# A decoder layer on one core: GpSimd's low-part split one step later than ScalarE's rounding, and the cross-attention's pieces spread over three passes

## What is computed

```
q, k, v = x @ Wq, x @ Wk, x @ Wv           # 16 heads of 128
q, k    = rmsnorm(q), rmsnorm(k)
a       = softmax(q @ k.T / sqrt(128) - slope[h] * distance, causal)
y       = rmsnorm(a @ v);   x1 = layernorm(x + concat(y) @ Wproj)
cross   = softmax((ctx @ Wq2.T + bq) @ (ctx @ Wk2.T + bk).T)    # needs the context alone
x2      = layernorm(x1 + x1 @ cross.T)
h       = sigmoid(bit(x2, w_gate)) * bit(x2, w_up);  out = layernorm(x2 + bit(h, w_down))
```

## Time and profile before

| | |
|---|---|
| median of 3 runs | 456.12 us |
| the profiled execution, its own time | 455.92 us |
| its span, first to last instruction | 454.1 us |
| TensorE matmul / weight load busy | 90% / 81% |
| VectorE, ScalarE, GpSimd busy | 71%, 59%, 42% |
| chain of waits, by engine | TensorE 68%, issue 11%, GpSimd 10%, VectorE 6%, ScalarE 2% |

### The profile page before, as it was taken

One profiled execution on the slowest core, in us unless ns is written; L12 is line 12 of the kernel. 1 busy time (PEld: TensorE's weight loads), 2 busy tenths in 40 slices (PEclk: granted clock), 3 DMA queues, 4 the chain that ended last, 5 costly groups with the idle time before them and its releaser, 6 DMA issues.

```text
span 454.1 us, 9089 instructions
## 1 busy us (share of the span) xinstructions
PE 408.9 (90%) x2602; PEld 366.2 (81%) x2612; DVE 320.5 (71%) x1002; ACT 268.7 (59%) x752; POOL 190.1 (42%) x298
## 2 busy tenths in 40 slices
PE   3787999888999999999999999999999999997462
PEld 3666877777899998889999989999999898995221
DVE  2265667676886878887768787877677878973673
ACT  3376756675766646677566466675555567663051
POOL 2536464656444543334435433344345433341201
PEclk9999999999999999999999999999999999999885
DMA  7996535331720333444302443335004444000000
GB/s 215 341 329 221 183 125 210 113 132 69 280 71 0 94 122 136 140 139 133 102 1 70 137 131 113 117 133 162 1 7 141 135 139 139 3 14 12 0 1 23
DMA packets 28736, 52.62 MB, mean 116 GB/s; under 512 B 2576, under 2 KB 22288, under 8 KB 28688
## 3 DMA queue, kind: packets, MB, share of 16 engines
q1 hardware_dynamic: 27968, 52.04, 34.3%
q10 hardware_dynamic: 720, 0.00, 0.1%
HBM read 41.55 MB, written 10.49 MB: 115 GB/s over the span
## 4 chain that ended last, share of the span: by engine, by line
PE 68%; issue 11%; POOL 10%; DVE 6%; ACT 2%; SPq 1%; DMA 1%; POOLq 0%; DVEq 0%; ACTq 0%
PE ps L518 23%; PE ps L571 10%; PE ps L532 5%; PE ps L547 5%; PE ps L538 4%; POOL qk_rstd L378 4%; POOL w_hl L359 4%; PE ps L491 3%; PE ps L552 3%; PE ps L554 3%; PE ps L553 3%; PE ps L546 3%; PE ps L560 2%; POOL y_rstd L386 2%; PE ps L500 2%
## 5 line engine op out<-in xcount | busy, mean ns | idle before, releaser
L518 PE MATMUL ps<-w_hl,xT_hi 128*128 128x384 f32 x512 | 150.9, 376 | 6.3 <-DVE qk_n L750 3.6
L378 POOL TENSOR_TENSOR qk_rstd<-qk_sum,minus_half 128x2 f32<-128x2 f32 x128 | 92.5, 723 | 121.7 <-DVE qk_sum L756 121.3
L518 PEld LDWEIGHTS ps<-w_hl,xT_hi 128*128 128x128 f32 x512 | 91.6, 193 | 14.8 <-issue 9.8
L659 ACT ACTIVATE sq<-ps 128x256 f32<-128x256 f32 x128 | 49.1, 384 | 73.2 <-PE ps L518 71.9
L756 DVE TENSOR_REDUCE qk_sum<-sq 128x2 f32<-128x258 f32 x128 | 53.7, 419 | 49.6 <-ACT sq L659 49.3
L518 PE MATMUL ps<-w_hl,xT_lo 128*128 128x384 f32 x256 | 87.8, 343 | 0.0
L750 DVE TENSOR_TENSOR qk_n<-ps,qk_rstd 128x256 f32<-128x256 f32 x128 | 54.2, 424 | 42.7 <-POOL qk_rstd L378 40.1
L386 POOL TENSOR_TENSOR y_rstd<-y_sum,minus_half 128x2 f32<-128x2 f32 x64 | 47.8, 747 | 67.8 <-DVE y_sum L904 67.8
L571 PE MATMUL ps<-wp,yT 128*128 128x256 f32 x256 | 65.7, 380 | 0.0
L707 ACT ACTIVATE sqy<-ps 128x258 f32<-128x258 f32 x64 | 24.7, 386 | 42.2 <-PE ps L554 42.2
L518 PEld LDWEIGHTS ps<-w_hl,xT_lo 128*128 128x128 f32 x256 | 49.2, 192 | 0.0
(11 more groups left out here) (127 smaller groups left out, 754.6 us busy)
## 6 DMA issues: line engine op xcount, KB each, us to landing
w_hl<-w_store SPq DMA_DIRECT2D x36, 768.0 KB, 4.3
w_store<-w_hl SPq DMA_DIRECT2D x12, 768.0 KB, 4.0
w_raw<-in_L_attn_Wq SPq DMA_DIRECT2D x16, 128.0 KB, 3.0
w_raw<-in_L_attn_Wk SPq DMA_DIRECT2D x16, 128.0 KB, 3.0
w_raw<-in_L_attn_Wv SPq DMA_DIRECT2D x16, 128.0 KB, 3.4
wp<-in_L_attn_Wproj SPq DMA_DIRECT2D x4, 512.0 KB, 6.5
ff_raw<-in_L_ffn_w_gate SPq DMA_DIRECT2D x1, 1024.0 KB, 7.1
ff_raw<-in_L_ffn_w_up SPq DMA_DIRECT2D x1, 1024.0 KB, 9.8
```

The source lines that it names most:

```text
L378: pool.tensor_tensor(qk_rstd[:, t, :], qk_sum[:, t, :], minus_half[:], ALU.pow).then_inc(s_rs[t], 1)
L518: last = pe.matmul(ps[:, t, 0:3 * D], xa[:, k, tok], w_hl[:, place(h), wa, k * 3 * D:(k + 1) * 3 * D], start=(i == 0), stop=(i == len(part ...
L659: act.activation(sq[:, t, :, 0:D], ps[:, t, 0:2 * D].rearrange("p (a d) -> p a d", a=2), ACT.Square).then_inc(s_sq[t], 1)
```

## The change

The low part of head n+1 (not n+2) is split in step n of GpSimd, so it reads a high part that ScalarE rounded in step n-1. On ScalarE the rounding moves behind the second `squares`; the exponentials of the energies move ahead of it, and EN now stands in place "b" of the step before, with `norm_cross` one step later. Eight pieces move out of the first pass: CQ, CK of batches 2 and 3, EN, AT, XT of batch 2 to steps 16 to 20, and EN, AT, XT of batch 3 to steps 31 to 34. The first pieces move one step earlier. FF goes to place "a" (but one), its clamp to the start of VectorE's step, its unrounding to the end of the step before. The loop over the first two roundings (`LEAD` is 2) is the same work.

```
--- before.py
+++ after.py
@@ -39,15 +39,16 @@
 BANK = 512
 
 
-FF_STEP = 6
+FF_PLACES = ((6, "a"), (7, "a"), (8, "b"), (9, "a"), (10, "a"), (11, "a"), (12, "a"), (13, "a"), (14, "a"), (15, "a"),
+             (16, "a"), (17, "a"))
 
 
 def filler_plan(batches, heads):
-    plan = [(1, "a", "XW", 0), (1, "b", "CT", 0), (2, "a", "CT", 1), (2, "b", "CQ", 0), (3, "a", "CK", 0),
-            (4, "a", "EN", 0), (4, "b", "WS", 0), (5, "a", "AT", 0), (5, "b", "XT", 1), (6, "a", "EN", 1),
-            (7, "a", "AT", 1), (8, "a", "CQ", 1), (9, "a", "CK", 1), (10, "a", "EN", 2), (11, "a", "AT", 2),
-            (12, "a", "EN", 3), (13, "a", "AT", 3), (14, "a", "XT", 2), (15, "a", "XT", 3)]
-    plan += [(FF_STEP + i, "b", "FF", i) for i in range(12)]
+    plan = [(0, "a", "XW", 0), (0, "b", "CT", 0), (1, "a", "CT", 1), (1, "b", "CQ", 0), (2, "a", "CK", 0),
+            (3, "b", "EN", 0), (5, "a", "WS", 0), (5, "b", "AT", 0), (7, "b", "EN", 1), (9, "b", "AT", 1),
+            (11, "b", "XT", 1), (16, "b", "CQ", 1), (17, "b", "CK", 1), (18, "b", "EN", 2), (19, "b", "XT", 2),
+            (20, "b", "AT", 2), (31, "b", "EN", 3), (33, "b", "AT", 3), (34, "b", "XT", 3)]
+    plan += [(n, slot, "FF", i) for i, (n, slot) in enumerate(FF_PLACES)]
     tail = [(1, "a", "X", 0), (1, "b", "M", 0), (2, "a", "X", 1), (2, "b", "M", 1), (3, "b", "Q", 0),
             (4, "a", "G0", 0), (4, "b", "U0", 0), (5, "a", "G1", 0), (5, "b", "U1", 0), (6, "a", "Q", 1),
             (6, "b", "G0", 1), (7, "a", "U0", 1), (7, "b", "G1", 1), (8, "a", "U1", 1), (8, "b", "H", 0),
@@ -384,13 +385,13 @@
                     pool.wait_ge(s_ssy, n - 2)
                     wait(pool, s_yn, n - 3)
                     pool.tensor_tensor(y_rstd[:], y_sum[:], minus_half[:], ALU.pow).then_inc(s_ry, 1)
-                if n < H - LEAD:
-                    split_lo(n + LEAD, 0)
+                if LEAD <= n + 1 < H:
+                    split_lo(n + 1, 0)
                 if live[0]:
                     qk_pow(0, n)
-                if n < H - LEAD:
-                    split_lo(n + LEAD, 1)
-                    split_lo(n + LEAD, 2)
+                if LEAD <= n + 1 < H:
+                    split_lo(n + 1, 1)
+                    split_lo(n + 1, 2)
                 if b >= 0 and s == 0:
                     ln_pow(0, 2 * b)
                 if b >= 0 and s == 2:
@@ -588,8 +589,8 @@
 
             act.wait_ge(s_xT, 1)
             act.copy(xT_hi[:, :, 0:T], ps[:, 0, :].rearrange("p (k t) -> p k t", k=KC)).then_inc(s_xhi, 1)
-            w_hi(0)
-            w_hi(1)
+            for h in range(LEAD):
+                w_hi(h)
 
             def exponentials(b, bank):
                 act.wait_ge(s_xmax, b + 1)
@@ -689,12 +690,12 @@
                     act.activation(qT[:], ps_qT, ACT.Copy, scale=qk_scale)
                     act.activation(kT[:], ps_kT, ACT.Copy, scale=1.0 / SLOPE[(n - 1) % H]).then_inc(s_qkT, 1)
                 consume(n, "a")
+                if (n - 1, "b") in PLAN and PLAN[n - 1, "b"][0] == "EN":
+                    exponentials(PLAN[n - 1, "b"][1], PLAN[n - 1, "b"][3])
+                if live[0]:
+                    squares(1, n)
                 if n < H - LEAD:
                     w_hi(n + LEAD)
-                if live[0]:
-                    squares(1, n)
-                if (n, "a") in PLAN and PLAN[n, "a"][0] == "EN":
-                    exponentials(PLAN[n, "a"][1], PLAN[n, "a"][3])
                 if 2 <= n < 5:
                     sum_ff(n + 1)
                 if b >= 0 and s == 7:
@@ -895,7 +896,7 @@
                 if b < 0:
                     s = -1
                 A, A2 = 2 * b, 2 * b + 1
-                ff = n - FF_STEP
+                ff = [m for m, _ in FF_PLACES]
                 if live[1]:
                     norm(1, n - 1)
                 if live[3]:
@@ -904,10 +905,10 @@
                     dve.tensor_reduce(y_sum[:], sqy[:], AX.X, ALU.add).then_inc(s_ssy, 1)
 
                 consume(n - 1, "b")
-                if 0 <= ff < 12:
-                    unround_ff(ff)
-                if (n - 1, "a") in PLAN and PLAN[n - 1, "a"][0] == "EN":
-                    norm_cross(PLAN[n - 1, "a"][1])
+                if n in ff:
+                    quantise_ff(ff.index(n))
+                if (n - 2, "b") in PLAN and PLAN[n - 2, "b"][0] == "EN":
+                    norm_cross(PLAN[n - 2, "b"][1])
                 if s == 0:
                     residual0(A)
                 if s == 1:
@@ -932,8 +933,6 @@
                     norm(0, n)
 
                 consume(n, "a")
-                if 0 <= ff < 12:
-                    quantise_ff(ff)
                 if s == 0:
                     residual0(A2)
                 if s == 3:
@@ -956,8 +955,9 @@
 
                 if 1 <= n < 4:
                     sum_ff(n - 1)
-                if 0 <= ff + 1 < 12:
-                    scale_ff(ff + 1)
+                if n + 1 in ff:
+                    scale_ff(ff.index(n + 1))
+                    unround_ff(ff.index(n + 1))
                 if s == 0:
                     normed(0, A, x1[:, 0])
                 if s == 2:
```

## The result

The changed kernel takes 435.21 us (median of 4 runs, 433.64 to 437.14) against 455.63 us in the same comparison: a ratio of 0.956, interval 0.950 to 0.961. 443 was forecast, with a range from 435 to 451: the direction and the cause were right, and the gain of 20.4 us is half as large again as the forecast 12.9, so that the time lies only 0.2 us inside the range. The profiled execution took 437.14, the longest of the four, with a span of 435.3.

A forecast was written before the change was run, and what follows sets the result against it. GpSimd's power, in order behind a split piece waiting for ScalarE's rounding, was taken to bound the first pass. 12.2 + 6.1 + 1.7 - 4.6 - 2.0 - 0.5 = 12.9; 455.92 - 12.9 = 443 us, range 435 to 451.

The forecast's parts named there:

- Steps 6 to 13: First pass, eight steps: GpSimd's wait for the rounding goes, 61.31 us become 49.1, gain 12.2, bounds 7 and 15.3.
- the 1.6 for late clamps: Steps 6 to 13: FF block in place "a" waits for a clamp VectorE has just made, 0.2 a step, 1.6 us.
- the 1.5 around EN: Steps 6 to 13, around EN of batch 1: VectorE's division (0.69) and maximum in a step keeping FF work, 1.5 us.
- The walk along step 17: Step 17, an FF step without splitting, as model: split pieces nearly fit GpSimd's idle times, low part about 0.7 us early.
- Steps 0 to 5: Start of first pass: earlier power, fewer gaps, earlier clock rise; 44.20 us become 38.1, gain 6.1, bounds 3 and 8.7.
- 3.8 for the sums of absolute weights: Steps 0 to 5: waits kept for VectorE's sums in two steps (2 x 1.1) and ScalarE's last sum (1.6).
- Steps 14 and 15: Without two XT pieces and a late start, 12.80 us become 11.1, gain 1.7, bounds 1.0 and 1.7.
- The moved pieces: Second and third pass: TensorE pays eight pieces, 4.6 us, plus 2.0 for step 20 and 0.5 for exponentials and bank readers.
- step 20: VectorE has batch 0's residuals plus batch 2's division and low part, with a wait: 2.0 us lost, bounds 0.5 and 3.5.
- TensorE waiting for the low part: Rival: VectorE late, so TensorE's next projection stands 0.6 us in each of 13 split steps, 8 us, 451; chance 0.09.
- Blocked ports: Rival: FF operations on VectorE stand a whole split piece, twice a step in nine steps, 9 us, 452; chance 0.06.
- The floor: Whole kernel: all bounds on the good side, gain 20.6 us, 435; chance 0.04.

The follow-up runs named there:

- experiment 3: Changed kernel with the split back in the step of its rounding and the rounding back ahead of the second squares, pieces in new places: 455.36 us, ratio 0.999.
- experiment 1: Kernel before with one part of the change, GpSimd splitting head n+1 in step n, all else as before: 435.27 us, ratio 0.955.
- experiment 10: Kernel before with only GpSimd splitting head n+1 in step n, the same code as experiment 1, run again: 436.39 us, ratio 0.956.
- experiment 5: Changed kernel with the first five pieces (XW, two CT, CQ, CK) one step later, as they stood before: 435.88 us, ratio 0.955.
- experiment 6: Changed kernel with batch 2's pieces (CQ, CK, EN, XT, AT) one step earlier: 433.64 us, ratio 0.950.
- experiment 7: Kernel of experiment 6 with EN and AT of batch 3 moved from steps 31 and 33 to steps 64 and 66: 436.41 us, ratio 0.956.
- experiment 9: The changed kernel once more, unaltered: 435.57 us, ratio 0.956.

## Why the prediction was right, and where it was off

**The bound: right.** GpSimd's in-order wait set the first pass. The lag alone gives it all, and with the wait kept (experiment 3) nothing is gained. The direction and the mechanism were forecast; the size came out 1.6 times the forecast, and that 435.21 still lies in the range is luck.

**Steps 6 to 13: 12.2 forecast, 14.85 measured**, near the bound of 15.3. The 46.0 for TensorE alone was right (46.46); the 1.6 for late clamps and the 1.5 around EN did not come. The walk along step 17 held: power at 2.4 us, low part 1.6 ahead of need (0.7 was forecast), rounding under cover.

**Steps 0 to 5: 6.1 forecast, 10.55 measured, outside the bounds of 3 and 8.7.** This is the term that failed, in both of its parts. TensorE's rests fell from 8.3 us to 1.7, where I kept 3.8 for the sums of absolute weights on VectorE and ScalarE; with the lag alone they are 2.7 (experiment 1) and, from this window, 3.2 (experiment 10), which is near the 3.8:

```profile
7.94:43.62 35.68, 32.50 (x191) 28.71 (x191) 24.16 (x71) 26.81 (x72) 21.35 (x30) 1.00 0.99 315
```

And TensorE's work fell from 35.94 to 31.96, where I took 1.2 off for the clock, 2.5 at most: its projections run at the upper level from about 13 us instead of 21.6. XT explains 0.4 of these 4.0. Part of it is chance of one execution: with the lag alone the same work took 34.07 in one and 32.50 in the other. I expected fewer gaps to bring the rise forward; experiment 5 has the gap of 0.38 and the early rise, and no run shows what sets it.

**Steps 14 and 15:** 1.7, as forecast. **The moved pieces:** 7.1 forecast, 7.12 measured over the later passes, with step 20 the tight one: its 7.14 us is 1.86 over a clean step, 1.16 of it the wait that experiment 6 takes away. The total is better than its parts: beyond AT's own time (0.5, by step 33) step 20 lost 1.3, where I took 2.0, and the rest came to 5.8, where I took 5.1.

**What the sum hid.** The moved pieces were booked as a cost against the lag's gain; the first pass gains as much from being rid of them, 7.5 us with the lag (step 16 starts at 106.71 and at 99.19; 6.5 by the repeats, 105.64 and 99.12) and 7.5 without. Half of the change is a wash: TensorE pays a piece wherever it never rests. Experiment 1, expected at 440, came to 435 mainly by the same term that failed above, steps 0 to 5, and not by steps 6 to 13.

**The rivals.** TensorE waiting for the low part did not come, with a margin of 1.6 us. The split runs in 14 steps, not in the 13 of its price.

*Blocked ports.* I misread the rows. The Trainium skill (SBUF — State Buffer, "Who interferes with whom") says that whichever engine issues first holds the pair of ports that VectorE and GpSimd share for the whole instruction, while the other fully blocks. For the split the traces agree: a clamp that begins under a piece of the split ends 0.28 us after the end of that piece, in all 19 cases of the kernel before, the changed kernel and experiment 1. Under GpSimd's power on 128x2 they do not: in experiment 3 a clamp at 67.30, with such a power running from 66.86 to 67.75, took 0.41, its length alone. A case of the split in the changed kernel, then one of experiment 1 (its row has two pieces, to 61.42):

```profile
54.24 0.73 POOL L360 TENSOR_TENSOR w_hl<-w_raw,w_hl 128x256 fp32r<-128x256 f32 x1
54.48 0.78 DVE L786 TENSOR_SCALAR ff_q<-ff_round 128x512 bf16<-128x512 f32 x1
```

```profile
59.99 1.43 POOL L359 TENSOR_TENSOR w_hl<-w_raw,w_hl 128x256 fp32r<-128x256 f32 x2
61.06 0.64 DVE L785 TENSOR_SCALAR ff_q<-ff_round 128x512 bf16<-128x512 f32 x1
```

So the 0.18 of step 9 comes of a piece that was nearly half done, not of a weak block: a block costs less than what is left of the piece, not a whole 0.68 twice a step. In the changed kernel only 2 of 12 clamps meet a piece (0.78 and 0.59 us; the one of step 9 took 0.42). In experiment 1 nine do, at 0.58 to 0.70 us, eight of them in steps 6 to 13, where TensorE never rests: there the block costs no time.

*The floor*, 435, given 0.04, is where the time fell, though not by its terms: steps 0 to 5 gave more than its 8.7, and the moved pieces cost more than its 5.1. The waits that I kept in reserve were one by one plausible and together too many.

## What to carry to other kernels

Where an engine runs its list in order, look for a wait that stands ahead of work which is already ready, and let the waiting work read its operand one step old: pointing three calls at another head gave 20 us here, and no work was removed. A piece of work costs its own time on an engine that never rests, wherever it stands; moving it paid here only out of a step in which another engine is late (experiment 6). Rests in a drain at the end are no room for it where they lie in a chain: there two pieces cost more than they freed (experiment 7).

## What the runs showed of the hardware

The moment at which TensorE reaches its upper level varies between executions of equal code: in the kernel of experiments 1 and 10 the projection took 0.52 us a matmul still at 14.55 in one execution and 0.34 by 12.90 in the other, and TensorE's work in steps 0 to 5 took 34.07 and 32.50 us.

At the end of the kernel the granted clock differs from run to run of equal work: the changed kernel's last stretch took 51.99 us at 0.75 in its first profile and 48.89 at 0.86 in that of experiment 9. So 3 us of a single profile's span say nothing of the change.

A VectorE clamp that begins under a piece of GpSimd's split (0.73 us) ends 0.28 us after that piece: in the kernel before, the changed kernel and experiment 1 it took 0.58 to 0.78 us instead of 0.42.
